# First scores from the upper halves of the float32 queries, and rounded keys summed by GpSimd instead of written by ScalarE

## What is computed

```python
x = x + tanh(g_xattn[0]) * xattn(layernorm(x), ctx, ctx)       # q from x, k and v from the context
x = x + tanh(g_ffn[0]) * ffn(layernorm(x))

# xattn
scores = einsum('bhqd,bhkd->bhqk', qh, kh) / sqrt(8)
probs  = softmax(scores, axis=-1)
out    = einsum('bhqk,bhkd->bhqd', probs, vh) @ W_o + b_o      # heads put back together first

# ffn: expert idx = argmax(gates), weighted with the largest gate
o = gelu(x @ W1[idx] + b1[idx]) @ W2[idx] + b2[idx]
```

## Time and profile before

| | before |
|---|---|
| median of 3 runs | 354.69 us (352.94 to 355.47) |
| profiled execution | 356.73 us |
| its span, first to last instruction | 355.0 us |
| TensorE busy | 300.8 us, 85% |
| VectorE busy | 285.4 us, 80% |
| ScalarE busy | 252.8 us, 71% |
| GpSimd busy | 231.1 us, 65% |
| granted TensorE clock, mean | 0.968 |

### The profile page before, as it was taken

How to read it: one execution, slowest core, us unless ns; L and a number is a source line. 1 busy time by engine, 2 the same in 40 slices (tenths; PEclk the granted TensorE clock), 3 DMA queues, 4 the chain that set the end, 5 groups by cost and what they waited for, 6 DMA issues and landing times.

```text
span 355.0 us, 16204 instructions
## 1 busy us (share of the span) xinstructions
PE 300.8 (85%) x6014; PEld 223.6 (63%) x6014; DVE 285.4 (80%) x1025; ACT 252.8 (71%) x651; POOL 231.1 (65%) x372
## 2 busy tenths in 40 slices
PE   2968899998999898999898787667988999999940
PEld 1535666665675665666665655456777999999830
DVE  7777999899998999999999799988777666666610
ACT  3766799989999889998998795767443555555410
POOL 6493654184498885798188643277777777777771
PEclk9998999999999999999999898999999999999985
DMA  5354345344313322423121112421135543433110
GB/s 118 84 172 151 92 144 175 86 142 104 96 58 122 123 67 78 143 67 118 54 74 59 67 61 75 118 71 60 49 94 141 139 118 109 110 101 101 57 41 0
DMA packets 47160, 34.05 MB, mean 96 GB/s; under 512 B 9800, under 2 KB 42955, under 8 KB 47083
## 3 DMA queue, kind: packets, MB, share of 16 engines
q1 hardware_dynamic: 42440, 23.90, 23.9%
q0 software_dynamic: 4352, 9.00, 7.6%
q10 hardware_dynamic: 292, 0.13, 0.1%
HBM read 17.13 MB, written 10.04 MB: 77 GB/s over the span
## 4 chain that ended last, share of the span: by engine, by line
PE 43%; DVE 22%; ACT 17%; issue 10%; POOL 3%; DMA 2%; ACTq 1%; POOLq 0%; DVEq 0%; SPq 0%
PE m L1366 10%; PE sc L1338 8%; DVE mx L1054 6%; ACT PT L633 4%; PE sc L1199 4%; ACT PT L631 3%; ACT dev L561 3%; PE sc L1209 3%; PE sc L1192 3%; PE m L1428 3%; DVE TV L1063 2%; PE m L1363 2%; PE pv L1274 2%; PE sc L1326 2%; DVE NV L1074 2%
## 5 line engine op out<-in xcount | busy, mean ns | idle before, releaser
L1054 DVE TENSOR_REDUCE mx<-sc 128x8 f32<-128x512 f32 x128 | 81.9, 682 | 14.0 <-PE sc L1209 13.7
L439 POOL DMA_INDIRECT records<-XR,pos x64 | 62.7, 979 | 35.2 <-DVE XR L926 17.5
L498 POOL DMA_INDIRECT out<-fo,rr x71 | 70.3, 990 | 21.5 <-issue 20.0
L631 ACT ACTIVATE PT<-sc 128x512 f32<-128x512 f32 x64 | 38.2, 597 | 19.1 <-issue 13.2
L380 POOL TENSOR_TENSOR rstd<-ve,mhalf 128x4 f32<-128x4 f32 x16 | 16.7, 1041 | 53.3 <-DVE ve L769 53.2
L1366 PE MATMUL m<-w,fgT 128*128 x280 | 49.0, 298 | 0.1
L1033 DVE SCALAR_TENSOR_TENSOR fo<-m,rr 128x128 f32<-128x128 f32 x70 | 24.5, 350 | 27.2 <-PE m L1366 26.9
L1338 PE MATMUL sc<-fxT,w1s 128*128 128x128 f32 x276 | 43.3, 279 | 3.1 <-DVE w1s L1025 2.7
L1274 PE MATMUL pv<-PT,V 128*32 128x64 f32 x2048 | 42.9, 223 | 1.1 <-DVE NV L1074 0.7
L614 ACT ACTIVATE fxT<-sc 128x128 f32<-128x128 f32 x69 | 19.2, 278 | 30.2 <-PE sc L1326 30.2
L1199 PE MATMUL sc<-Qd,kT 32*128 32x128 f32 x1024 | 40.3, 274 | 0.0
(11 more groups left out here) (229 smaller groups left out, 695.8 us busy)
## 6 DMA issues: line engine op xcount, KB each, us to landing
rr<-records SPq DMA_DIRECT2D x71, 72.0 KB, 2.0
XC<-in_x SPq DMA_DIRECT2D x16, 256.0 KB, 4.4
C<-in_ctx SPq DMA_DIRECT2D x16, 256.0 KB
Qd<-Qf SPq DMA_DIRECT2D x64, 64.0 KB
Kd<-kb SPq DMA_DIRECT2D x64, 32.0 KB, 2.2
w<-in_L_ffn_W SPq DMA_DIRECT2D x16, 128.0 KB, 3.4
out<-fo,rr POOLq DMA_INDIRECT x71, 2.3
w1l<-in_L_ffn_W SPq DMA_DIRECT2D x8, 128.0 KB, 3.9
```

The costliest lines, as they stand in the source:

```text
L439: nc.gpsimd.indirect_dma_start(out=records, out_offset=bass.IndirectOffsetOnAxis(ap=pos[:, u:u + 1], axis=0), in_=XR[:, u, :], in_offset=N ...
L498: nc.gpsimd.indirect_dma_start(out=out_rows, out_offset=bass.IndirectOffsetOnAxis(ap=rr[q][:, R_ID:R_ID + 1].bitcast(U32), axis=0), in_=fo ...
L631: nc.scalar.activation(pt[:, 0:2], sc[:, 0:2, 256:512], ACT.Exp)
L1054: nc.vector.tensor_reduce(mx[c % 2][:, t:t + 2, HI * u:HI * u + HI], sc[:, t:t + 2, 0:256].rearrange("p t (i k) -> p t i k", i=HI), AX_X, ...
```

## The change

The bfloat16 queries are no longer written. The first scores read the upper 16 bits of each float32 query instead, as a view with a step of two bfloat16 elements; this is a truncated value instead of a rounded one. `Qf` becomes two buffers, since it is now read by the first scores of four tiles. In steps 2 to 15 the bfloat16 keys are no longer written by ScalarE from PSUM: GpSimd adds the two masked float32 copies in `kT` and writes the sum as bfloat16 into `kb`. It does so between the deviation and the xn of the next step's norm. Steps 0 and 1 keep ScalarE's copy. TensorE's value projections no longer wait for `kb` from step 2 on.

```diff
-        Qf = sb("Qf", [P, CT])
-        qb = [sb(f"qb{i}", [P, CT], BF16) for i in range(2)]
+        Qf = [sb(f"Qf{i}", [P, CT]) for i in range(2)]
+        qb = [q[:, :].bitcast(BF16).rearrange("p (t two) -> p t two", two=2)[:, :, 1] for q in Qf]
...
-                    sp.dma_start(Qd[s % 3][i::HI, i // 2, :], Qf[i::HI, :]).then_inc(qd_in[s % 3], 16)
+                    sp.dma_start(Qd[s % 3][i::HI, i // 2, :], Qf[s % 2][i::HI, :]).then_inc(qd_in[s % 3], 16)
...
+            def rounded_keys(s):
+
+                pool.wait_ge(kT_ok, s + 1)
+                pool.wait_ge(kd_in[(s - 1) % 2], 16 * HI * ((s - 1) // 2 + 1))
+                k = kT[s % 3][:, :, :, :, :].rearrange("r u b p k -> r (u b) p k")
+                nc.gpsimd.tensor_tensor(kb[:, :].rearrange("r (a k) -> r a k", k=S), k[:, :, 0, :], k[:, :, 1, :],
+                                        ALU.add).then_inc(kb_ok, 1)
+
             def norm(c):
                 deviation(c)
+                if c >= 3:
+                    rounded_keys(c - 1)
...
                     norm(s + 1)
+                if s + 1 == NC:
+                    rounded_keys(s)
...
             def keys(s):
                 act.wait_ge(k_ps, s + 1)
                 if s >= 1:
-                    act.wait_ge(kd_in[(s - 1) % 2], 16 * HI * ((s - 1) // 2 + 1))
+                    act.wait_ge(kd_in[0], 16 * HI)
...
                 if j == 1 and 1 <= s < NC:
-                    keys(s)
+                    if s == 1:
+                        keys(s)
+                    else:
+                        act.wait_ge(k_ps, s + 1)
                     keys_turned(s)
                 if j == 2 and s < NC:
                     act.wait_ge(q_ps, s + 1)
                     if s >= 2:
                         act.wait_ge(s1_ps, CU * (s - 1))
-                    nc.scalar.activation(qb[s % 2][:, :], m0[:, :], ACT.Identity, bias=b16[:, 0:1], scale=ISC).then_inc(qb_ok, 1)
-                    if s >= 1:
-                        act.wait_ge(qd_in[(s - 1) % 3], 16 * HI * ((s - 1) // 3 + 1))
-                    nc.scalar.activation(Qf[:, :], m0[:, :], ACT.Identity, bias=b16[:, 0:1], scale=ISC).then_inc(qf_ok, 1)
+                        act.wait_ge(qd_in[(s - 2) % 3], 16 * HI * ((s - 2) // 3 + 1))
+                    nc.scalar.activation(Qf[s % 2][:, :], m0[:, :], ACT.Identity, bias=b16[:, 0:1], scale=ISC).then_inc(qf_ok, 1)
...
-                        pe.wait_ge(qb_ok, c + 1)
+                        pe.wait_ge(qf_ok, c + 1)
...
-                    pe.wait_ge(kb_ok, s + 1)
+                    if s < 2:
+                        pe.wait_ge(kb_ok, s + 1)
```

More of the change, by code:

```diff
@@ L189, in gated_block @@
         q_ps, k_ps, v_ps = (sem(n) for n in ("q_ps", "k_ps", "v_ps"))
-        qb_ok, qf_ok, kb_ok, kT_ok, v_ok = (sem(n) for n in ("qb_ok", "qf_ok", "kb_ok", "kT_ok", "v_ok"))
+        qf_ok, kb_ok, kT_ok, v_ok = (sem(n) for n in ("qf_ok", "kb_ok", "kT_ok", "v_ok"))
         kd_in = [sem(f"kd_in{i}") for i in range(2)]
```

## The result

| | before | after |
|---|---|---|
| median of 4 runs | 355.08 us (352.94 to 356.96) | 373.62 us (371.45 to 1421.44) |
| ratio, with its 95% interval | | 1.0492 [1.0439, 1.0544] |
| profiled execution, its span | 356.73, 355.0 us | 373.15, 371.4 us |
| end of the main loop's last exponential (L633; now L645) | 241.5 us | 258.1 us |
| TensorE, VectorE busy | 300.8, 285.4 us | 305.3, 289.2 us |

The changed kernel is slower, by 4.4 to 5.4%. One of its four runs took 1421 us and is no part of the ratio; the median of the other three is 373.15 us. A second batch, on a chip of the same pace, gave 1.0443 [1.0343, 1.0542] for the same kernel. The forecast was 364.4 us with a range of 358 to 373. The sign was right; the forecast loss, 9.7 us, is a little more than half of the measured one (1.0492 of 355.08 us is 372.6 us, 17.5 us more), and the result lies at the upper edge of the range.

The account below looks back on a forecast made before the run. Bound: the TensorE-VectorE-ScalarE ring (3.03 us), ScalarE in the keys' slot (3.28), then late Kd. Ordinary steps 3.2 + 1.2, steps 8, 11, 14 2.7 + 2.7 + 0.7, roomy steps -0.8: +9.7 on 354.69, 364.4 us, range 358 to 373.

Parts of the forecast that it names:

- The keys' second chain: Rounded keys, SyncE's four Kd scatters, next step's first scores on TensorE: 2.9 us spare before; keys 2.90 us later in step 10.
- ScalarE's relief: Slot with the keys, without ScalarE's rounded copy, falls from 3.28 to 3.03 us: 0.26 a step, 3.6 over 14 steps.
- L: Time from first issue to last landing of the four Kd scatters: 3.6 us at best, up to 4.4 or 5.4.
- ordinary steps: Main-loop steps stalled by late Kd: +0.8 us each in steps 3 to 6, +0.3 each in 7, 9, 10 and 13.
- L - 3.7: Growth in us of an ordinary step, from Kd's scatter time, gain of 0.26 included; never less than -0.26.
- Steps 8 and 11: GpSimd's backlog of record sends ahead of the sum delays Kd: +2.7 us each.
- Step 3: Main-loop step priced by Kd's lateness only, loads behind the scatters having about a step: +0.8 us.
- Steps 14 and 15: Step 14: eight records, but more room, +0.7 us; step 15: room, keeps the gain, -0.8 together with steps 2 and 12.
- The rule on the ports: GpSimd and VectorE share SBUF ports: one 0.24 us VectorE delay in each of 14 steps, 3.4 us, not in the sum.
- Faster: Rival: Kd still lands in time and ScalarE's saved copy counts; 351 us if backlogs vanish too; chance 0.07.
- Ports: Rival: port delays (3.4 us) or strided loads (3 us) besides late Kd, in every tile: 16 us, 371; chance 0.12.
- GpSimd's xn late: Rival: GpSimd's four xn, feeding TensorE's next transposes, come 1.28 us later; hidden behind Kd's stall, no time of its own.

Follow-up runs that it names:

- the unused sum: Kernel before plus the same GpSimd sum into a tile nobody reads, ScalarE still writing the keys: 1.0010 in the first batch, 359.28 us, 1.0079 in the second.
- the scatters that wait for it: Kernel before plus a GpSimd sum nobody reads, with SyncE's Kd scatters held until that sum is done: 469.85 us, 1.0220.
- the sum moved back: Changed kernel with GpSimd's sum of the keys behind the whole norm of the next group: 492.54 us against 460.31, 1.0737.
- the queries: Kernel before with only the queries' half of the change (two Qf buffers, strided view), ScalarE's keys kept: 459.53 us, 1.0017.
- the second profile: Changed kernel run again, unaltered, in the second batch: 372.80 us against 356.71, 1.0443.
- sum first: Changed kernel with GpSimd's sum of the keys ahead of the deviation instead of behind it: 368.09 us, 1.0247.
- the keys alone: Kernel before with only the keys' half of the change, ScalarE still writing the rounded queries: 467.17 us, 1.0192; in the second batch 374.14 us, 1.0466.

## Why the prediction was right or wrong

**The bound and the sign: right.** The keys' second chain had 2.9 us to spare, the round through GpSimd takes 2.6 to 2.9 us more (4.9 and 5.0 in steps 8 and 11) and L grows, and Kd becomes late. That the main cause is Kd's time and neither GpSimd's work nor ScalarE's is shown by the unused sum (1.0079 where the changed kernel has 1.0443), by the scatters that wait for it (1.0220 against 1.0010 in one batch) and by the sum moved back.

**The queries, the strided view, the sum's length: right.** 1.0017 for the queries, 104 ns for a load, 1.27 us for the sum where 1.28 was taken from the earlier trace rows.

**ScalarE's relief: right that it is hidden.** The slot with the keys went from 3.28 to 3.03 or 3.04 us in steps 3, 4, 8 and 11 alone and stayed at 3.14 to 3.27 in the other ordinary ones; what was gained the first scores took back.

**L in ordinary steps: too small.** I took 4.5 in steps 3 to 6 and 4.0 later. Measured from first issue to first scores, where these waited, it was 4.38, 5.53, 4.52 and 4.53 in steps 4 to 7, and 4.61, 4.27, 4.79 and 4.63 in steps 9, 10, 12 and 13, 4.7 on average. The formula, L - 3.7, held in step 10 (4.27 gives 0.57, and it grew by 0.48), but not everywhere: over the eight steps it gives about 7.6 us with the measured L, and they grew by 4.5. Part of each stall was taken back in other slots, most in steps 9 and 12, and this was not followed up. The row of 3.6 us was the best case (3.7 is reached in steps 8 and 11 and with the sum last, where the loads were issued 8 us earlier); the four issues alone take 2.4 to 3.3 us. The eight steps had been put at 3.3 us; the unused sum costs 2.1 there, so that 3.3 and 4.5 come so close is partly luck: T(5) is not L. One sum of the prediction is off in itself: with L = 3.6 everywhere the steps with a backlog would be 0.4 us cheaper each as well, +3.3 and not +4.5, so the low end is 358.

**Steps 8 and 11: right in mechanism, 0.9 us too much together.** 5.4 forecast, 4.5 measured. The sum stands behind the records, as said, and L was 3.7 where 4.0 was taken. Step 11 was 3.0 for 2.7. Step 8 was 1.5 for 2.7: giving it step 11's number without its own rows was the mistake.

**Step 3: wrong.** 0.8 forecast, 4.2 measured. (In the second profile it is 1.5; the 2.9 more ahead of it lie where the clock is halved, so that the two sums agree at 16.7 and 17.0 is in part chance.) The step that failed is the sentence "Qd is first read six slots after Kd, and the loads behind it have about a step, so only Kd matters". The loads' own readers did have time. What I did not ask is what else shares the DMA engines with loads that start 2 us later: here, as far as the profiles tell, TensorE's instructions, with a pause of 1.1 to 2.9 us.

**Steps 14 and 15: wrong.** 0.4 forecast, 4.1 measured. The rule on the ports was weighed, priced at 3.4 us as a rival, and left out of the sum "since the addition runs after ve and beside reductions and transposes whose operands are mostly in PSUM". That holds for ordinary steps. In the steps with routing work VectorE has a chain of small instructions with operands in SBUF, and that chain, not Kd, is what sets the end there; the hits shown cost 0.5 to 1.4 us each, not the 0.24 of `ve` in the earlier trace rows. The unused sum measures this term by itself: 4.2 us in the profile, 2.8 us by the ratio, about the rival's price by another way. The hit in step 15, in the changed kernel:

```profile
221.43 1.26 POOL L404 TENSOR_TENSOR kb<-kT 128x512 bf16<-128x512 f32 x1 [5.08 <-ACT kT L618]
```

```profile
221.49 1.22 DVE L987 TENSOR_TENSOR tl<-edge 128x8 f32<-128x8 f32 x1
```

It explains 1.0 of the 2.2 us of that period (0.17 us without the sum). The other 1.2 us are not settled; 6.8 us at half the clock lie there (233.4 to 240.2), where the kernel before has 3.4 us and the kernel with the unused sum none:

```profile
233.40:240.20 6.80, 6.12 (x141) 0.50 0.34 83
```

**What stood in its stead, in one line:** 16.7 - 9.7 = 7.0 us, of which 3.4 are step 3, 3.6 steps 14 and 15, 1.2 ordinary steps, and -0.9 steps 8 and 11, -0.3 ahead of T(3). The range was reached by luck: its upper end stood for a larger L or for ports in every tile, and most of what was missing came from step 3 and from steps 14 and 15.

**Rivals.** Faster: refuted, Kd was late in ten steps and no form of the change was faster. Strided loads: no cost (104 ns). Ports: real, but in a few steps, not in every tile. GpSimd's xn late: in the changed kernel it stays hidden behind Kd's stall, as said; with Kd in time, in the kernel with the unused sum, it shows twice:

```profile
PE m L1418 <- POOL xn L415: 2.0, 2, 1.1
```

## What to carry to other kernels

A copy that ScalarE makes from PSUM can stand at the head of a chain with its own deadline: before it goes to another engine, compute when its last reader's data lands, with L taken from the busiest step and not from the quietest. Ask of every queue that is pushed back what lies behind it, even where its readers have time; here a late burst of loads went with a pause of TensorE in the middle of a group. And an extra GpSimd instruction is to be laid against the small SBUF-only instructions of VectorE, in the steps where those form the critical chain: here the hits cost 0.5 to 1.4 us each beside a sum of 1.27 us, whatever its own length. A comparison of single steps across chips holds only where the same kernel has been seen to agree on both.

## What was unexpected of the hardware

- TensorE stood 1.1 to 2.9 us in the middle of a group without waits, in each of seven profiles in which a 16 KB instruction packet started 4.4 to 5.6 us after T(3), and in none of seven in which it started by 3.0 us.
- After the pause of 2.86 us the granted clock fell to 0.50 for 3.4 us, and 32 matmuls (L1442) took 1.98 us there instead of 1.15 in step 10. After one of 2.93 us ("sum first") it stayed at 1.00.
- A copy of eight columns took 1.65 us and a product with eight columns 1.22 us on VectorE under a GpSimd sum of 1.27 us, each ending within 0.1 us of it.
- Chips differ: the same kernel with the unused sum has a span of 359.1 us on one and 455.4 us on another, equal up to 100 us. Between 100 and 200 us TensorE executed 2447 matmul instructions on the first and 1795 on the second:

```profile
100.00:200.00 100.00, 89.32 (x2447) 61.36 (x2435) 94.27 (x318) 89.44 (x221) 82.46 (x136) 1.00 0.27 87
```

```profile
100.00:200.00 100.00, 80.92 (x1795) 52.53 (x1786) 66.50 (x230) 67.39 (x164) 63.73 (x105) 0.88 0.22 70
```

(first the chip where before takes 357 us, then the one where it takes 459; columns: PE, PE's loads, DVE, ACT, POOL busy, granted clock, DMA share, GB/s). The same change weighs differently on them: the keys alone cost 4.7% on the one and 1.9% on the other. Why TensorE pauses there was not studied.
